# Cross-attention and mixture-of-experts layer: x^T by a second load and a block transpose on VectorE, layer norm 1 folded into the query weights and the exponential

## The chip, the cores and the metric

One core of a Trainium2 chip runs the kernel. The metric is the device time of one execution in microseconds (us); the profile is of one further execution. The engines are TensorE (PE, with its weight loads as PEld), VectorE (DVE), ScalarE (ACT), GpSimd (POOL) and SyncE (SP), which issues most DMAs. Each runs its own instructions in order and waits for the others by semaphores.

## The reference

There are 64 batches. A batch is x, 256 rows by 256 columns, and a context of 77 rows by 192. All is float32.

```python
def layernorm(x): return (x - mean(x)) / sqrt(var(x) + 1e-5)      # over the 256 columns

def cross_attention(x, context, Wq, Wk, Wv, Wo, bo):               # 8 heads of 64
    q, k, v = x @ Wq, context @ Wk, context @ Wv                   # split into heads
    attn = softmax((q @ k.T) * 64 ** -0.5)
    return (attn @ v) @ Wo + bo

def ffn(h, sim_matrix, gates, q_proj, k_proj, v_proj, o_proj):     # 16 experts of 64
    rw = gating(h, sim_matrix, gates)        # softmax over the experts that are on, at least the two best
    q, k, v = [sum_e rw[:, e] * (h @ proj[e]) for proj in (q_proj, k_proj, v_proj)]
    attn = softmax(causal(q @ k.T / 8)) @ v
    return sum_e (rw[:, e] * attn) @ o_proj[e]

x = x + cross_attention(layernorm(x), ctx, ...)
x = x + ffn(layernorm(x), ...)
```

## The kernel before

A product of two float32 matrices is made as three fast ones: each operand is split in a high half (rounded, written by ScalarE with a copy) and a low half (VectorE subtracts the high half from the source), and TensorE adds lo x hi, hi x lo and hi x hi (`product`, L577). Keys and values are folded into weights for three batches at a time: `gq` is the query weight times the keys of each head (jobs `g`, from `wq` and jobs `k`), `uo` the values times Wo (jobs `u`, from jobs `v`), so that the scores of a batch are xn @ gq and its cross-attention output is probs @ uo. These go through DRAM (`g_dram`, `u_dram`).

The main loop has steps i = 1 to 65. In step i the attention of batch i + 1 runs (scores S0 to S3, softmax, transposes PT0 to PT2 of the probabilities, output Y), the first half of the expert projections of batch i, the second half and the causal attention of batch i - 1, and the last product of batch i - 2. Each engine has its own list of this work, written by hand (`step` in each block), so the order on each queue is fixed.

Layer norm 1 of batch i + 2 (`nxt`) also runs in step i. VectorE takes mean and variance of the loaded tile `xt` (`ln1_a`), GpSimd raises the variance to the power -0.5 (`power`, L1822) and makes the shift, ScalarE writes the normalised rows `xn` (`ln1_b`, L1152, into the memory of `probs`; instructions L1149), TensorE transposes them in four pieces in slot XT (`a_xT`, L645; instructions L649) into PSUM, ScalarE copies the high half from there (L1021) and VectorE subtracts the low half (L1419). SP loads `xt` with one DMA (L412).

Slots of TensorE's work for attention and for the jobs share three PSUM banks in turn, in the order of `A_ORDER` (L42): E0, S0 to S3, E1, E2, PT0, PT1, PT2, E3, M1, XT, M2, M3, Y, L1, L2. A slot waits (`freed`, L588) until the slot three places back has been read out. So M2 gets the bank of E3, PT2 that of E2, and Y that of XT. Which job stands in a slot depends on i % 3 (`JOBS`, L44): E1 holds a `k` job for i % 3 == 2, which ScalarE reads out with four copies (L1036 to L1039) and VectorE with two subtractions (L1433), and a `g` or `u` job else, with one copy (L1082, L1105) and one subtraction (L1460, L1466). M3 holds a job (`ct`, the context's transpose) for i % 3 == 1 alone.

The expert projections are `b_qkv` j = 0 to 15; their blocks are accumulated by VectorE (L1541), or for the first two by ScalarE (L1142). The sum of attention and residual is VectorE's `a_y` (L1493). The causal attention's last product is `c_pv` on TensorE, into bank_c; it needs the low half of the transposed probabilities, VectorE's `c_pT` (L1547). The row maximum of the scores is taken by VectorE (`a_s`, L1471); ScalarE makes the 16 exponentials of a batch (`a_exp`, L1112), four a block, with the maximum as bias. `c_mix` (L1582) scales the attention output for all experts, and GpSimd subtracts its low half (L1915). GpSimd adds the bias `bo` to the rows of x (`a_xb`, L1842).

## Time and profile before

| | us |
|---|---|
| median of 3 runs | 2549.08 (2548.26 to 2549.45) |
| the profiled execution | 2547.88 |
| its span, first to last instruction | 2546.1 |

The span is followed in slices of 1/40. Each digit below is the busy share of a slice in tenths (9 is 90% or more); PEclk is the granted clock of TensorE in tenths of full speed; DMA is the mean busy share of the 16 DMA engines.

```profile
PE   5799999999999999999999999999999999999997
PEld 5799999999999999999999999999999999999997
DVE  6788888888888888888888888888888888888885
ACT  6666666666666666666666666666666666666642
POOL 2244444444444444444444444444444444444442
PEclk8899999999999999999999999999999999999998
DMA  6765556465565556466565556465565556465531
```

Times in the profile are us from the start of the span unless marked ns. In the rows "idle before" is how long the engine had stood, and the name behind the arrow is what ended that. The work is even from the third slice to the last but one. A share is a mean over stages with different limits.

### The profile page before, as it was taken

How to read it: one execution, taken by the hardware profiler on the slowest of the kernel's cores; microseconds unless marked ns; L12 is line 12 of the kernel's file. 1: busy time of each engine (PE TensorE's matmuls, PEld its weight loads, DVE VectorE, ACT ScalarE, POOL GpSimd, SP SyncE). 2: the span in 40 equal slices, each digit the busy share in tenths (PEclk: the TensorE clock that was granted, in tenths of full speed). 3: DMA queues.
4: the chain of work that ended last, by engine and by line, in shares of the span. 5: the costliest groups of instructions: out<-in, count | busy, mean ns of one | idle time of the engine just before them, and what ended most of it. 6: DMA issues, size and time to landing. Idle time of an engine off the chain costs nothing.

```text
span 2546.1 us, 54414 instructions
## 1 busy us (share of the span) xinstructions
PE 2477.4 (97%) x17308; PEld 2427.1 (95%) x17308; DVE 2124.1 (83%) x6126; ACT 1584.3 (62%) x5126; POOL 1104.3 (43%) x1741
## 2 busy tenths in 40 slices
PE   5799999999999999999999999999999999999997
PEld 5799999999999999999999999999999999999997
DVE  6788888888888888888888888888888888888885
ACT  6666666666666666666666666666666666666642
POOL 2244444444444444444444444444444444444442
PEclk8899999999999999999999999999999999999998
DMA  6765556465565556466565556465565556465531
GB/s 180 232 184 178 170 164 197 153 198 184 163 188 178 169 165 197 153 198 183 163 189 177 170 165 197 148 203 182 165 189 176 170 165 197 154 194 180 162 108 46
DMA packets 288070, 441.48 MB, mean 173 GB/s; under 512 B 20356, under 2 KB 199492, under 8 KB 279723
## 3 DMA queue, kind: packets, MB, share of 16 engines
q1 hardware_dynamic: 218155, 369.84, 44.6%
q10 hardware_dynamic: 69632, 68.17, 11.1%
q8 instruction: 140, 2.29, 0.4%
q14 instruction: 143, 1.17, 0.1%
HBM read 254.86 MB, written 181.83 MB: 172 GB/s over the span
## 4 chain that ended last, share of the span: by engine, by line
PE 81%; DVE 7%; POOL 5%; issue 3%; ACT 3%; DMA 0%; POOLq 0%; SPq 0%; DVEq 0%; ACTq 0%
PE bank_b L581 12%; PE bank_b L582 12%; PE bank_b L583 12%; PE bank_c L581 5%; PE bank_c L582 5%; PE bank_c L583 5%; PE bank_a L581 4%; PE bank_a L582 4%; PE bank_a L583 4%; PE bank_a L726 3%; PE bank_a L690 2%; PE bank_a L702 2%; DVE both L1433 2%; PE bank_a L691 1%; PE bank_a L665 1%
## 5 line engine op out<-in xcount | busy, mean ns | idle before, releaser
L1541 DVE SCALAR_TENSOR_TENSOR acc<-bank_b,rw,acc 128x192 f32<-128x192 f32 x1792 | 653.2, 408 | 108.9 <-PE bank_b L583 106.6
L581 PE MATMUL bank_b<-wqkv_hi,x2T_lo 128*128 128x384 f32 (+1 forms) x2048 | 721.3, 352 | 3.0 <-ACT acc L1142 1.6
L582 PE MATMUL bank_b<-wqkv_lo,x2T_hi 128*128 128x384 f32 (+1 forms) x2048 | 694.4, 339 | 0.0
L583 PE MATMUL bank_b<-wqkv_hi,x2T_hi 128*128 128x384 f32 (+1 forms) x2048 | 690.4, 337 | 0.0
L1915 POOL TENSOR_TENSOR mixs_lo<-mix,mixs_hi 128x512 fp32r<-128x512 f32 x254 | 378.2, 1520 | 164.5 <-ACT mixs_hi L1220 164.5
L1112 ACT ACTIVATE probs<-bank_a,s_max 128x77 f32<-128x77 f32 x1024 | 317.9, 331 | 202.3 <-DVE s_max L1471 202.3
L581 PEld LDWEIGHTS bank_b<-wqkv_hi,x2T_lo 128*128 128x128 f32 x2048 | 387.0, 189 | 5.4 <-ACT acc L1142 2.2
L582 PEld LDWEIGHTS bank_b<-wqkv_lo,x2T_hi 128*128 128x128 f32 x2048 | 387.5, 189 | 0.0
L583 PEld LDWEIGHTS bank_b<-wqkv_hi,x2T_hi 128*128 128x128 f32 x2048 | 385.5, 188 | 0.0
L1220 ACT ACTIVATE mixs_hi<-mix 128x512 fp32r<-128x512 f32 x256 | 159.8, 633 | 208.8 <-DVE mix L1582 208.8
L581 PE MATMUL bank_c<-wo_hi,mixs_lo 128*128 128x256 f32 x1000 | 281.2, 281 | 3.7 <-POOL mixs_lo L1915 3.7
L582 PE MATMUL bank_c<-wo_lo,mixs_hi 128*128 128x256 f32 x1000 | 280.5, 280 | 0.0
L583 PE MATMUL bank_c<-wo_hi,mixs_hi 128*128 128x256 f32 x1000 | 280.3, 280 | 0.0
L1908 POOL TENSOR_TENSOR probs<-probs,p_sum 128x616 f32<-128x616 f32 x128 | 156.1, 1220 | 249.7 <-DVE p_sum L1478 249.7
L1582 DVE TENSOR_TENSOR mix<-rw_all,late_tiles 128x512 f32<-128x512 f32 x256 | 245.9, 1000 | 20.3 <-ACT late_tiles L1214 20.3
L1889 POOL TENSOR_TENSOR mix<-acc 128x192 f32<-128x192 f32 x128 | 76.1, 595 | 377.9 <-DVE acc L1541 377.9
L1832 POOL TENSOR_TENSOR pow_out<-pow_in,expo 128x2 f32<-128x2 f32 (+1 forms) x128 | 111.3, 869 | 243.6 <-DVE pow_in L1391 227.2
L1112 ACT ACTIVATION_READ_ACCUMULATOR probs<-bank_a,s_max 128x1 f32 x1024 | 215.0, 210 | 0.0
L581 PEld LDWEIGHTS bank_c<-wo_hi,mixs_lo 128*128 128x128 f32 x1000 | 189.2, 189 | 3.8 <-issue 3.8
L582 PEld LDWEIGHTS bank_c<-wo_lo,mixs_hi 128*128 128x128 f32 x1000 | 189.2, 189 | 0.0
L583 PEld LDWEIGHTS bank_c<-wo_hi,mixs_hi 128*128 128x128 f32 x1000 | 189.1, 189 | 0.0
L581 PE MATMUL bank_a<-uo,pT_lo 128*128 128x256 f32 x630 | 177.3, 281 | 0.2 <-DVE xT_lo L1419 0.2
(262 smaller groups left out, 6389.7 us busy)
## 6 DMA issues: line engine op xcount, KB each, us to landing
gq<-g_dram SPq DMA_DIRECT2D x63, 1232.0 KB, 5.7
rw_all<-rw_dram ACTq DMA_DIRECT2D x128, 512.0 KB, 6.8
uo<-u_dram SPq DMA_DIRECT2D x63, 1024.0 KB
g_dram<-draft SPq DMA_DIRECT2D x103, 462.0 KB
u_dram<-draft SPq DMA_DIRECT2D x127, 308.0 KB
g_dram<-mixs_lo SPq DMA_DIRECT2D x63, 462.0 KB
xt<-in_x_dram SPq DMA_DIRECT2D x64, 256.0 KB, 4.7
out_dram<-mix SPq DMA_DIRECT2D x62, 256.0 KB, 4.0
```

Source lines behind the costliest of these rows:

```text
L581: nc.tensor.matmul(dst, lhs[1], rhs[0], start=start, stop=False)
L582: nc.tensor.matmul(dst, lhs[0], rhs[1], start=False, stop=False)
L583: return nc.tensor.matmul(dst, lhs[0], rhs[0], start=False, stop=stop)
L726: last = nc.tensor.transpose(bank_pt(n, k)[0:rows, col * P:(col + 1) * P], probs[:, t, chunk * P:chunk * P + rows], ident[:, :])
L1112: last = nc.scalar.activation(probs[:, t, h * NC:(h + 1) * NC], bank_s(n, j)[:, k * NC:(k + 1) * NC], ACT.Exp, bias=s_max[:, j, k:k + 1], ...
L1220: nc.scalar.activation(mixs[0][:, 2 * j:2 * j + 2, :], mix[:, 2 * j:2 * j + 2, :], copy).then_inc(mix_hi, 1)
L1541: V.scalar_tensor_tensor(acc[:, t, k, :], src, rw[:, t, e:e + 1], acc[:, t, k, :], ALU.mult, ALU.add).then_inc(b_evac, 1)
L1582: V.tensor_tensor(mix[:, 2 * j:2 * j + 2, :], rw_all[:, 2 * j:2 * j + 2, :], aT2[:, :].unsqueeze(1).to_broadcast([P, 2, T]), ALU.mult).the ...
L1832: G.tensor_tensor(dst, src, expo[:, 0:m], ALU.pow).then_inc(ln_pow[k], 1)
L1889: G.tensor_tensor(qkv[:, t, :], acc[:, t, 0, :], acc[:, t, 1, :], ALU.add).then_inc(qkv_ready, 1)
L1908: G.tensor_tensor(part, part, p_sum[:, half, 1, :, :].unsqueeze(3).to_broadcast([P, NT, HB, NC]), ALU.mult).then_inc(p_ready, 1)
L1915: G.tensor_tensor(mixs[1][:, 2 * j:2 * j + 2, :], mix[:, 2 * j:2 * j + 2, :], mixs[0].bitcast(F32)[:, 2 * j:2 * j + 2, :], ALU.subtract).t ...
```

## The change

x^T no longer comes from TensorE. SP loads x a second time with four DMAs of 64 KB (`load_blocks`), so that partitions 32k to 32k + 31 hold the rows s, s + 32, ... of the k-th quarter of the columns; the pieces are 64 columns (256 B) long. VectorE's transpose of 32 x 32 blocks (`a_blocks`) turns this tile into x^T in SBUF (`x_cols`), where even columns come first and odd ones second; Wq is loaded in the same order of rows. ScalarE's copy and VectorE's subtraction then read SBUF, not PSUM. Both stand later in the step: the block transpose behind `c_s`, the copy behind `b_exp`, the subtraction behind `a_y`. The loads stand between slots E2 and E3 on SP and wait for PT2's transposes, since they go into the memory of `probs`.

Layer norm 1 is no longer applied to x. Its mean goes into the query weights: each column of `wq` is centred, once at the start (four sums and four multiplies on VectorE, a bias in ScalarE's copies). Its deviation becomes a factor of the scores of a row: (var + eps) x 64 to the power -0.5 is the scale of the exponential, a column of SBUF, and one more multiply on VectorE scales each maximum. `ln1_b` and the shift on GpSimd are gone. Slot XT has no work and holds no bank; Y now waits for PT2's.

```diff
+        x_cols, x_later = [probs[:, :, :].rearrange("p t c -> p (t c)")[:, s * CC * T:(s + 1) * CC * T] for s in range(2)]
+        TB = T // 32
+        x_first = x2_first[:, :, :].rearrange("p t c -> p (t c)")
...
             def load_x(n):
                 if n:
                     sp.wait_ge(xb_ready, at(1, n - 1, 0))
-                    sp.wait_ge(ln_done[0], at(NT, n - 1, NT - 1))
+                    sp.wait_ge(ln_stats[0], at(2 * NT, n - 1, NT - 1))
...
+            def load_blocks(n):
+                if n > 1:
+                    sp.wait_ge(pt_fill, at(3, n - 1, 2))
+                for k in range(4):
+                    sp.dma_start(x_blocks(n)[k * 32:(k + 1) * 32, :].rearrange("p (k c) -> p k c", k=TB),
+                                 x[n, :, :].rearrange("(k s) c -> s k c", s=32)[:, :, k * C // 4:(k + 1) * C // 4]).then_inc(xt_in[n % 2], 16)
...
                 turn(i, "E2")
+                if on(i + 2):
+                    load_blocks(i + 2)
                 turn(i, "E3")
...
-            def a_xT(n):
-                pe.wait_ge(ln_done[0], at(NT, n, NT - 1))
-                for cc in range(CC):
-                    for t in range(NT):
-                        last = nc.tensor.transpose(bank_xt(n)[:, cc * T + t * P:cc * T + (t + 1) * P],
-                                                   xn[:, t, cc * P:(cc + 1) * P], ident[:, :])
-                last.then_inc(xt_fill, 1)
...
                 turn(i, "M1")
-                fill("XT", nxt, a_xT)
                 turn(i, "M2")
...
             def query_weights():
                 for k in range(HB):
                     act.wait_ge(wq_fill, k + 1)
-                    nc.scalar.activation(wq[:, 2 * k:2 * k + 2, :].rearrange("p a b -> p (a b)"), (banks_b[1:3] + banks_c)[k][:, :], copy,
-                                         scale=SCALE).then_inc(wq_hi, 1)
+                    act.wait_ge(wq_mean_ready, k + 1)
+                    for e in range(2):
+                        last = nc.scalar.activation(wq[:, 2 * k + e, :], (banks_b[1:3] + banks_c)[k][:, e * C:(e + 1) * C], ACT.Identity,
+                                                    bias=wq_mean[:, 2 * k + e:2 * k + e + 1])
+                    last.then_inc(wq_hi, 1)
 
             def a_xT(n):
                 act.wait_ge(xt_fill, at(1, n, 0))
-                nc.scalar.activation(xT[0][:, :, :].rearrange("p a b -> p (a b)"), bank_xt(n)[:, :], copy).then_inc(xt_hi, 1)
+                if n:
+                    act.wait_ge(s_fill, at(2 * NT, n - 1, 2 * NT - 1))
+                nc.scalar.activation(xT[0][:, :, :].rearrange("p a b -> p (a b)"), x_cols, copy).then_inc(xt_hi, 1)
...
-                                                bias=s_max[:, j, k:k + 1], accum_out=p_sum[:, half, 0, t, k:k + 1])
+                                                bias=s_max[:, j, k:k + 1], scale=pow_out[0][:, 0, t:t + 1], accum_out=p_sum[:, half, 0, t, k:k + 1])
...
                 do(ahead, a_pT, 2)
-                do(nxt, ln1_b)
                 turn(i, "E3")
                 do(now, b_xT, 0)
                 do(now, b_xT, 1)
                 turn(i, "M1")
-                do(nxt, a_xT)
                 do(before, c_qk)
                 turn(i, "M2")
                 do(before, c_exp)
                 do(now, b_exp)
+                do(nxt, a_xT)
                 turn(i, "M3")
...
             def query_weights():
                 for k in range(HB):
+                    dve.wait_ge(wq_fill, k + 1)
+                    mean = wq_mean[:, 2 * k:2 * k + 2]
+                    V.tensor_reduce(mean, (banks_b[1:3] + banks_c)[k][:, :].rearrange("p (e c) -> p e c", e=2), AX.X, ALU.add,
+                                    negate=True).then_inc(wq_sum, 1)
+                    dve.wait_ge(wq_sum, k + 1)
+                    V.tensor_scalar(mean, mean, 1.0 / C, None, ALU.mult).then_inc(wq_mean_ready, 1)
...
-                V.tensor_scalar(minus[k][:, :], mv[k][:, :, 0], -1.0, None, ALU.mult).then_inc(ln_var[k], 1)
                 if k == 0:
-                    V.tensor_scalar(pow_in[k][:, 0, :], mv[k][:, :, 1], EPS, None, ALU.add).then_inc(ln_var[k], 1)
+                    V.tensor_scalar(pow_in[k][:, 0, :], mv[k][:, :, 1], EPS, float(D), ALU.add, ALU.mult).then_inc(ln_var[k], 1)
...
+            def a_blocks(n):
+
+                dve.wait_ge(xt_in[n % 2], 64 * (n // 2 + 1))
+                if n:
+                    dve.wait_ge(pt_fill, at(3, n - 1, 2))
+                V.transpose(x_cols.rearrange("p (a k s) -> p a k s", a=CC, k=TB),
+                            x_blocks(n).rearrange("p (k r a) -> p a k r", k=TB, a=CC)).then_inc(xt_fill, 1)
+
             def a_xT(n):
                 hi, lo = flat(xT, slice(None), slice(None), slice(None))
                 dve.wait_ge(xt_hi, at(1, n, 0))
-                V.tensor_tensor(lo, bank_xt(n)[:, :], hi.bitcast(F32), ALU.subtract).then_inc(xt_evac, 1)
+                V.tensor_tensor(lo, x_cols, hi.bitcast(F32), ALU.subtract).then_inc(xt_evac, 1)
...
-                                negate=True).then_inc(s_max_ready, 1)
+                                negate=True).then_inc(s_top, 1)
+                dve.wait_ge(ln_pow[0], at(1, n, 0))
+                dve.wait_ge(s_top, at(2 * NT, n, j))
+                V.tensor_scalar(s_max[:, j, :], s_max[:, j, :], pow_out[0][:, 0, j % 2:j % 2 + 1], None, ALU.mult).then_inc(s_max_ready, 1)
...
                 turn(i, "M1")
-                do(nxt, a_xT)
                 do(now, b_z, 0)
...
                 do(before, c_s)
+                do(nxt, a_blocks)
                 do(before, c_p)
...
                 do(now, b_wsum)
                 turn(i, "M2")
                 do(ahead, a_y)
+                do(nxt, a_xT)
                 turn(i, "M3")
                 do(before, c_pT)
```

## Rows read from the trace of the kernel before

**Rows 1.** The page: busy us of each engine (share of the span), instructions.

```profile
PE 2477.4 (97%) x17308; PEld 2427.1 (95%) x17308; DVE 2124.1 (83%) x6126; ACT 1584.3 (62%) x5126; POOL 1104.3 (43%) x1741
```

**Rows 2.** Three steps: us, busy of PE, PEld, DVE, ACT, POOL, clock, DMA, GB/s.

```profile
974.00:1088.59 114.59, 114.15 (x809) 112.18 (x808) 97.60 (x285) 72.89 (x238) 51.48 (x81) 1.00 0.57 177
```

**Rows 3.** Timeline of PE around slot XT: start, us, line, out<-in.

```profile
1050.19 0.60 PE L649 MATMUL bank_a<-ident,probs 128*128 128x128 f32 x4
1050.84 0.37 PE L665 MATMUL bank_a<-cT_hi,wv_lo 128*128 128x232 f32 x1
```

**Rows 4.** Timeline of DVE in the same stretch; idle before in brackets.

```profile
1049.45 0.74 DVE L1541 SCALAR_TENSOR_TENSOR acc<-bank_b,rw,acc 128x192 f32<-128x192 f32 x2 [0.55 <-PE bank_b L583]
...
1050.11 0.68 DVE L1466 TENSOR_TENSOR mixs_lo<-bank_a,mixs_lo 116x512 fp32r<-116x512 f32 x1
```

**Rows 5.** Waits of PE's weight loads, 400 to 2400: total us, times, longest.

```profile
PEld bank_a L665 <- DVE mixs_lo L1460: 9.5, 36, 0.3
...
PEld bank_a L665 <- DVE mixs_lo L1466: 5.0, 17, 0.3
PEld bank_c L581 <- DVE mixs_lo L1547: 4.9, 17, 0.3
```

**Rows 6.** Timeline of DVE, second half of the step i % 3 == 0.

```profile
1019.02 0.17 DVE L1571 RECIPROCAL p_sum<-p_sum 128x2 f32<-128x2 f32 x1 [0.71 <-ACT mix L1185]
1019.22 0.60 DVE L1575 TENSOR_SCALAR mix<-mix,p_sum 128x128 f32<-128x128 f32 x2
1020.38 0.19 DVE L1527 TENSOR_REDUCE w_sum<-w 128x2 f32<-128x32 f32 x1 [0.55 <-POOL w L1874]
...
1021.50 0.69 DVE L1493 TENSOR_TENSOR late_tiles<-bank_a,xb 128x512 f32<-128x512 f32 x1
1022.27 0.56 DVE L1547 TENSOR_TENSOR mixs_lo<-bank_c,mixs_lo 128x384 fp32r<-128x384 f32 x1
```

**Rows 7.** One line's instructions: duration ns min/median/max.

```profile
L1582 DVE TENSOR_TENSOR mix<-rw_all,late_tiles x256: 682/693/1782, 145.8 to 2535.1; 128x512 f32<-128x512 f32 x128
```

**Rows 8.** Timeline of PE: the first product of c_pv in that step.

```profile
1023.13 0.28 PE L581 MATMUL bank_c<-mixs_lo,mixs_hi 128*128 128x256 f32 x1
```

**Rows 9.** ACT's groups by form: busy us, mean ns of one | idle before.

```profile
L1142 ACT ACTIVATE acc<-bank_b,rw 128x192 f32<-128x192 f32 x256 | 94.2, 425 | 99.4 <-POOL rw L1880 99.4
...
L1127 ACT ACTIVATE x2T_hi<-bank_b 128x256 fp32r<-128x256 f32 x128 | 42.3, 382 | 53.1 <-PE bank_b L763 53.1
L1021 ACT ACTIVATE xT_hi<-bank_a 128x512 fp32r<-128x512 f32 x64 | 38.0, 593 | 0.2 <-PE bank_a L649 0.2
```

**Rows 10.** Timeline of ACT, exponentials and E1, step i % 3 == 2.

```profile
1074.73 0.33 ACT L1112 ACTIVATE probs<-bank_a,s_max 128x77 f32<-128x77 f32 x1 [1.02 <-DVE s_max L1471]
...
1077.81 0.33 ACT L1112 ACTIVATE probs<-bank_a,s_max 128x77 f32<-128x77 f32 x1 [0.51 <-DVE s_max L1471]
...
1079.03 1.09 ACT L1149 ACTIVATE mix<-late_tiles,shift,pow_out 128x256 f32<-128x256 f32 x2
1080.29 0.36 ACT L1036 ACTIVATE only<-bank_a 64x231 fp32r<-64x231 f32 x1 [0.17 <-PE bank_a L669]
```

**Rows 11.** Timeline of DVE: E2's subtraction in the same step.

```profile
1083.89 0.63 DVE L1460 TENSOR_TENSOR mixs_lo<-bank_a,mixs_lo 128x462 fp32r<-128x462 f32 x1
```

**Rows 12.** Timeline of PE: transposes of slot PT2 in the same step.

```profile
1084.71 0.60 PE L726 MATMUL bank_a<-ident,probs 128*128 128x128 f32 x4
```

**Rows 13.** Timeline of DVE behind slot E1, step i % 3 == 1.

```profile
1044.73 0.74 DVE L1541 SCALAR_TENSOR_TENSOR acc<-bank_b,rw,acc 128x192 f32<-128x192 f32 x2 [0.81 <-PE bank_b L583]
```

**Rows 14.** The page's DMA queues: packets, MB, share of 16 engines.

```profile
q1 hardware_dynamic: 218155, 369.84, 44.6%
```

**Rows 15.** Timeline of SP's queue: issue of one load.

```profile
1061.76 0.40 SPq L412 DMA_DIRECT2D xt<-in_x_dram  x1
```

**Rows 16.** Timeline of PE in the opening: first use of the query weights.

```profile
21.61 0.35 PE L690 MATMUL bank_a<-both,wq 128*128 128x232 f32 x1 [2.90 <-issue]
```

**Rows 17.** Timeline of POOL behind the residual sum.

```profile
1060.44 1.30 POOL L1842 TENSOR_TENSOR xb<-xt,bo_all 128x512 f32<-128x512 f32 x1 [1.25 <-DVE late_tiles L1493]
```

81 lines of the change are left out of this document (37 added, 44 removed).

## The prediction

> **What bounds the kernel now.** I read the page's busy shares first: TensorE is busy for 97% of the span and VectorE for 83% [rows 1]. Then a window over three steps of the steady loop, since the work repeats with a period of three: 114.59 us, 38.20 a step, TensorE busy 114.15 of it at the full clock [rows 2]. So TensorE sets the end, and the change takes work from it. What it can give back must be read on TensorE's own timeline, at the place where the work goes, because a queue in order gives nothing back if its next instruction waits for something that is no earlier.
>
> **The four transposes, removed in 61 steady steps.** In the step shown they start at 1050.19 and the next product (L665, slot M2) starts at 1050.84 [rows 3], so the slot is worth 0.65 us, or 61 x 0.65 = 39.7 us at most. But the slots share three PSUM banks in turn: M2 gets the bank of E3 and waits until VectorE has subtracted that. That subtraction (L1466) starts at 1050.11 and lasts 0.68, so it ends at 1050.79 [rows 4], 0.05 before L665 starts. It follows the two accumulations of block 15, which themselves had waited 0.55 for TensorE [rows 4], so it is tied to a product ahead of the removed slot. The waits agree: within 2000 us the weight load of L665 waited for this subtraction 36 + 17 = 53 times, up to 0.3 us each [rows 5], which is every one of some 52 steps. The transposes stand in a hole that stays when they go. I credit 0.06 us a step (the longer start after a transpose), 61 x 0.06 = 3.7 us; bounds 0 and 39.7.
>
> **VectorE's subtraction that makes the low half, moved.** Before, it ran ahead of the router's maxima, where VectorE waits for TensorE. Now it stands right behind the residual sum (L1493) and ahead of the subtraction L1547, on which TensorE's product with V waits. In a step without context work L1493 starts at 1021.50 and L1547 at 1022.27, lasting 0.56 [rows 6]. The new one has two SBUF sources of 512 columns like L1582, whose shortest is 0.682 and median 0.693 [rows 7]; with the usual overlap of 0.08 it holds the engine for 0.61. L1547 then starts at 1021.50 + 0.61 + 0.61 = 1022.72 and ends at 1023.28, and the product, which started at 1023.13 [rows 8], starts near 1023.34 with a slower second one behind: +0.28 us. In the third of the steps that has context work in slot M3, L1547 is already the last to arrive (17 waits of up to 0.3 [rows 5]); so the whole 0.60 is added. Sum: 40 x 0.28 + 21 x 0.60 = 23.8 us. Lower bound 0, if something else on VectorE goes earlier; upper bound from the longest L1582, 1.782: 1.1 more in each of 61 steps, 67 us.
>
> **The exponential's scale.** Each of the 16 exponentials of a batch takes its scale from a column of SBUF instead of a constant. No row has this form. Nearest: L1142, 192 columns with such a scale, takes 425 ns, while L1127, 256 columns without, takes 382 [rows 9]; with L1021, 512 columns in 593 [rows 9], a column is 0.82 ns, 192 plain ones 329, and a scale column costs about 0.09 us (bounds 0 and 0.10). The maximum gets a multiply behind it that waits for it: L1571 to L1575, such a pair, are 0.20 us apart [rows 6], so each maximum reaches ScalarE 0.21 us later, and the fourfold adds 0.8 us a step to VectorE. In the step shown the second block of exponentials starts at 1074.73, the last at 1077.81 after an idle 0.51, and the layer norm behind them at 1079.03 [rows 10]. Now: second block at 1074.73 + 0.42 = 1075.15, then 12 exponentials by 0.39 in a row, 1079.86, so 0.83 later. Slot E1's copies started at 1080.29 after 0.17 of waiting for TensorE [rows 10], so they start 0.66 later. In steps of type i % 3 == 2 four copies stand there, VectorE waits for them and then has no gap until E2's subtraction, L1460 at 1083.89 for 0.63, end 1084.52 [rows 11]. TensorE's transposes PT2 need that bank and start at 1084.71 [rows 12]. With 0.07 from the end of a subtraction to its release the rest, 0.59 us, is a new wait: 20 x 0.59 = 11.8 us. In the other two types E1 has one copy, and behind it VectorE waits 0.81 for TensorE [rows 13], so nothing. Bounds 0 (no cost of the scale column) and 61 x 0.66 = 40 us.
>
> **VectorE's block transpose.** No row shows one. From below, one pass over 512 columns, the 0.68 of L1582; from above two passes, 1.35. I take 0.68, as its neighbours with 512 columns all take one pass. It stands behind c_s, where VectorE idles 0.71 before L1571 [rows 6]: nothing at 0.68, and up to 1.2 is covered in two of three types by its next wait, 0.55 for GpSimd (L1527) [rows 6]. ScalarE's copy to the high half moves behind b_exp, where that engine waits for GpSimd's weights: free. The normalising pair on ScalarE (L1149 on probs) goes, 1.08 us a step, from a place where the engine then waits for TensorE: no gain.
>
> **The second load.** 4 DMAs of 64 KB, 1024 pieces of 256 B a batch. Queue 1 spent 44.6% of 16 x 2546 us on 218155 packets [rows 14], 83 ns each at 1.7 KB, so at most 1024 x 83 / 16 = 5.3 us, and half of that if a packet's time goes down with its size. On SP the wait for PT2 holds back slot E3's store and what follows; an issue is 0.40 [rows 15], 1.6 for four, and E3's store is due only 4 us later. From PT2 (1085) to the block transpose one step on (1056.8 + 38.2 = 1095) are 10 us; issue, transfer and landing need 5 to 8. Free, with 2 us to spare. The Trainium skill (DMA: Bandwidth & Descriptors, Specifications) wants at least 512 B a transfer for line rate, with a read-modify-write below that; no row here shows such a load. By the rows it adds nothing to the sum, by that rule it comes nearer to its deadline, and past it the late-load rival below holds.
>
> **The opening.** Before the first use of the query weights (L690 at 21.61 [rows 16]) VectorE now makes four sums over 512 columns. At L1582's 0.69 [rows 7] and with the dependent multiply this is 0.81 a head pair, 3.3 us, with ScalarE's two copies in place of one hidden behind. The block transposes ahead of the copies of batches 0 and 1 add 0.5, their 32 longer exponentials (0.09 each) 2.7, and the missing normalisation gives back 1.0: +5.5 us (bounds 2 and 9).
>
> **The sum** against the profiled execution, 2547.88 us (span 2546.1 and 1.8 around it): -3.7 + 23.8 + 11.8 + 5.5 = +37.4, so 2585.3. The median of the runs is 1.2 above the profiled execution: **2586 us**, 1.4% slower.
>
> **The rivals.**
> Faster (0.13): the hole ahead of M2 closes, because E3's subtraction gets earlier by the 0.65. For it speaks that ScalarE loses 1.08 us just before E3's copy; against it that VectorE's accumulations ahead of it waited for TensorE. It decides at an end of L1466 by 1050.2 in the frame shown. With the new waits hidden too, 2549.1 - 39.7 + 5.5 = 2515 us (0.10); if they stay, 2515 + 23.8 + 11.8 = 2550 (0.03).
> Waits hidden, nothing gained (0.13): the subtraction's place and the scale column cost nothing on TensorE, only the opening counts: 2549.1 + 5.5 - 3.7 = 2551, or up to 2556 with a remnant. For it: the slack is misread by no more than 0.3 us a step.
> Port collision (0.10): the moved subtraction reads two SBUF tensors while GpSimd adds the bias to x (L1842, 1.30 us from 1060.44 [rows 17]), started by the same residual sum. L1582 shows the effect: 0.68 alone, 1.782 at worst beside GpSimd [rows 7]. In my sum VectorE is first, since its instruction follows without a gap. If GpSimd is first, up to 61 x 1.1 = 67 us more: 2653; with half of them 2620. The Trainium skill (SBUF — State Buffer, Who interferes with whom) calls the shared port pair an exclusive lock, taken by whoever starts first; by it, too, the order decides.
> Late load (0.06): the pieces land after the block transpose's turn, and VectorE stands, with the softmax's normalisation and the router's sum queued behind. 1 us a step would be 61 us, 2647.
> The forecast (0.58), with its own range of 2566 to 2606.
>
> **How the numbers follow.** The range must leave out no more than 2 in 10: it starts at 2549, above the faster rival (0.10) and an edge of the mixed form (0.02), and ends at 2615, leaving out half of the two last rivals (0.08). Faster by over 0.2% (about what a measurement of this kernel can tell from no change) comes from the first rival less its mixed form: 0.10. Within 0.2% (2544 to 2554): that mixed form and most of the hidden case, 0.13. Slower: 0.77.
>
> **What would show it.** The weight load of M2's product waits for E3's subtraction for some 0.7 us instead of 0.3. The product with V (bank_c) waits for L1547's successor in all steps, 0.3 to 0.9. In every third step PT2's transposes wait 0.6 for E2's subtraction. The exponentials stand 0.39 apart instead of 0.30. The block transpose takes 0.68 and VectorE never waits for the load. The first product with query weights starts near 25. I am wrong if M2 starts 0.6 earlier behind M1, if the product with V starts without a wait, or if VectorE or the load shows waits that I have not named.

## The result and the profile after

| | median of 4 runs, us | range |
|---|---|---|
| before | 2548.67 | 2546.77 to 2549.45 |
| after | 2634.56 | 2631.22 to 2636.62 |

The ratio is 1.034, with a 95% interval from 1.032 to 1.035: 86 us slower. The prediction was 2586 us, slower by 37, with 2615 as the upper end. The side was right, the size was not.

The page of the kernel after: busy us of each engine (share of the span), and its DMA queue 1.

```profile
PE 2489.9 (95%) x17052; PEld 2407.0 (92%) x17052; DVE 2183.6 (83%) x6390; ACT 1617.4 (62%) x5002; POOL 1109.4 (42%) x1677
...
q1 hardware_dynamic: 287659, 386.64, 47.5%
```

TensorE has 256 instructions fewer than in [rows 1] and yet falls from 97% to 95% of a longer span: it waits more. The page also follows the chain of work that ended last, from each instruction back to what released it. First the kernel before, then the kernel after, shares of the span:

```profile
PE 81%; DVE 7%; POOL 5%; issue 3%; ACT 3%; DMA 0%; POOLq 0%; SPq 0%; DVEq 0%; ACTq 0%
```

```profile
PE 35%; DVE 30%; issue 10%; ACT 9%; DMA 7%; POOL 5%; SPq 3%; DVEq 0%; ACTq 0%; POOLq 0%
```

Before, TensorE alone carried the chain; now VectorE carries nearly as much of it, and the loads 7%. The line numbers have moved: the product is now L598 to L600 (L581 to L583 before), E1's and E2's subtractions L1467, L1473 and L1440 (L1460, L1466, L1433), the one for the product with V L1557 (L1547), the transposes PT L732 (L726), the first products of M2 L671 (L665), the exponentials L1118 (L1112). New are the block load L423, the block transpose L1420, the moved subtraction L1426 and the multiply on the maxima L1482.

To find where the time went I laid a mark in every step, VectorE's residual sum (L1503, L1493 before), and read the stretches between two marks, windows of both kernels: us, busy of PE, PEld, DVE, ACT, POOL, clock, DMA, GB/s. First the kernel before. The stretches end in steps with i % 3 = 2, 0 and 1.

```profile
945.03:983.38 38.35, 38.18 (x271) 37.25 (x269) 32.81 (x97) 24.29 (x81) 17.14 (x27) 1.00 0.58 179
983.38:1021.50 38.12, 37.92 (x268) 37.25 (x268) 32.42 (x95) 24.13 (x81) 17.17 (x27) 1.00 0.56 171
1021.50:1059.60 38.10, 38.03 (x271) 37.65 (x271) 32.37 (x93) 24.46 (x81) 17.15 (x27) 1.00 0.58 182
```

And the same three of the kernel after.

```profile
981.53:1021.70 40.17, 38.44 (x264) 36.94 (x264) 33.91 (x100) 25.25 (x80) 17.21 (x26) 1.00 0.60 178
1021.70:1060.18 38.48, 37.81 (x264) 36.88 (x264) 33.23 (x98) 24.56 (x79) 17.26 (x26) 1.00 0.62 177
1060.18:1099.55 39.37, 38.45 (x267) 37.33 (x267) 33.12 (x98) 24.70 (x77) 17.25 (x26) 1.00 0.62 181
```

The first kind of stretch grows by 1.8 us, the second by 0.4, the third by 1.3. The clock is full in all of them. Over the run the mark of batch 3 comes at 196.38 instead of 180.84 (+15.5), from there to batch 60 there are 2243.11 instead of 2177.84 (+65.3), and from batch 60 to the last 115.27 instead of 111.49 (+3.8). Who makes TensorE wait in the steady part is seen in the waits of its weight loads, 400 to 2400: total us, times, longest.

```profile
PEld bank_a L671 <- DVE mixs_lo L1467: 22.3, 34, 0.7
PEld bank_c L598 <- DVE mixs_lo L1557: 21.4, 49, 0.6
PEld bank_a L708 <- DVE both L1440: 19.5, 34, 0.8
PEld bank_a L732 <- DVE mixs_lo L1467: 12.9, 17, 0.8
PEld bank_a L671 <- DVE mixs_lo L1473: 10.2, 17, 0.7
PEld bank_a L732 <- DVE both L1440: 8.4, 33, 0.7
```

Not all of this is new. Of the same list in the kernel before, one more row is needed beside [rows 5], the u jobs' (L702 there):

```profile
PEld bank_a L702 <- DVE both L1433: 7.7, 19, 0.6
```

L671 (slot M2) waits up to 0.7 instead of 0.3, which is the removed slot's time turned into waiting; the product with V (L598, bank_c) waits in nearly every step, not in every third; L732 (PT1 and PT2) waits for E1's and E2's subtractions, which it did not before; and L708 (the u jobs) waits 19.5 instead of 7.7, where the new part is slot L1's wait for M2's subtraction. M2's, PT2's and the product with V's were forecast, those of PT1 and L1 were not.

A new wait on VectorE tells why slot L1 is late. First SP's queue in the step whose block transpose is shown behind it, with i % 3 = 1, then VectorE, then TensorE at slot L1.

```profile
1047.59 1.88 SPq L423 DMA_DIRECT2D probs<-in_x_dram  x4
...
1085.21 0.80 SPq L451 DMA_DIRECT2D u_dram<-mixs_lo  x2
1086.06 4.99 SPq L423 DMA_DIRECT2D probs<-in_x_dram  x4
...
1097.18 0.71 DVE L1420 STREAM_TRANSPOSE probs<-probs 128x512 f32<-128x512 f32 x1 [1.23 <-DMA probs<-in_x_dram]
...
1098.73 0.78 DVE L1440 TENSOR_TENSOR both<-bank_a,only 64x231 fp32r<-64x231 f32 x2
...
1099.66 0.34 PE L708 MATMUL bank_a<-wo,both 128*116 128x256 f32 x1 [0.48 <-DVE both L1440]
```

The first row is the same load one step earlier, where no such stores stand ahead: 1.88 us for the four issues. Here they stand behind two stores of `u_dram` and take 4.99, where I had counted 1.6, and VectorE stands for 1.23 us until they have landed. In 17 such steps the four issues take 3.4 to 5.7 us, 4.5 in the middle; in the steps with i % 3 = 0 it is 1.8. Everything behind is late with it, down to the subtraction L1440 for which slot L1 waits.

### The profile page after: what moved, and what is told of

Read it like the earlier page. It is cut to its first block, busy times and chain, and to the rows that moved or that the text cites. A ratio compares the mean times of both kernels' runs of the same rounds, so it can differ in the third digit from the quotient of the medians.

```text
span 2629.4 us, 54494 instructions
## 1 busy us (share of the span) xinstructions
PE 2489.9 (95%) x17052; PEld 2407.0 (92%) x17052; DVE 2183.6 (83%) x6390; ACT 1617.4 (62%) x5002; POOL 1109.4 (42%) x1677
## 3 DMA queue, kind: packets, MB, share of 16 engines
q1 hardware_dynamic: 287659, 386.64, 47.5%
## 4 chain that ended last, share of the span: by engine, by line
PE 35%; DVE 30%; issue 10%; ACT 9%; DMA 7%; POOL 5%; SPq 3%; DVEq 0%; ACTq 0%; POOLq 0%
DVE acc L1551 8%; DMA probs<-in_x_dram 7%; PE bank_b L598 5%; PE bank_b L600 5%; PE bank_b L599 5%; DVE mix L1592 3%; DVE both L1440 3%; PE bank_c L598 3%; ACT probs L1118 3%; SPq L423 3%; PE bank_c L600 2%; PE bank_c L599 2%; DVE s_max L1478 2%; DVE s_max L1482 2%; ACT mix L1161 2%
## 5 line engine op out<-in xcount | busy, mean ns | idle before, releaser
L598 PE MATMUL bank_b<-wqkv_hi,x2T_lo 128*128 128x384 f32 (+1 forms) x2048 | 721.9, 353 | 3.2 <-ACT acc L1148 1.7
L600 PE MATMUL bank_b<-wqkv_hi,x2T_hi 128*128 128x384 f32 (+1 forms) x2048 | 693.3, 339 | 0.0
L1118 ACT ACTIVATE probs<-bank_a,s_max,pow_out 128x77 f32<-128x77 f32 x1024 | 410.3, 416 | 203.1 <-DVE s_max L1482 201.0
L598 PEld LDWEIGHTS bank_b<-wqkv_hi,x2T_lo 128*128 128x128 f32 x2048 | 387.8, 189 | 10.1 <-ACT acc L1148 6.7
L600 PEld LDWEIGHTS bank_b<-wqkv_hi,x2T_hi 128*128 128x128 f32 x2048 | 385.7, 188 | 0.0
L598 PE MATMUL bank_c<-wo_hi,mixs_lo 128*128 128x256 f32 x1000 | 282.3, 282 | 3.7 <-POOL mixs_lo L1930 3.7
L600 PE MATMUL bank_c<-wo_hi,mixs_hi 128*128 128x256 f32 x1000 | 283.9, 284 | 0.0
L1118 ACT ACTIVATION_READ_ACCUMULATOR probs<-bank_a,s_max,pow_out 128x1 f32 x1024 | 208.7, 204 | 0.0
L598 PEld LDWEIGHTS bank_c<-wo_hi,mixs_lo 128*128 128x128 f32 x1000 | 189.7, 190 | 3.9 <-issue 3.8
L600 PEld LDWEIGHTS bank_c<-wo_hi,mixs_hi 128*128 128x128 f32 x1000 | 188.5, 188 | 0.0
L1440 DVE TENSOR_TENSOR both<-bank_a,only 64x231 fp32r<-64x231 f32 x352 | 137.9, 392 | 47.6 <-ACT both L1045 43.7
```

Source lines behind the costliest of these rows:

```text
L598: nc.tensor.matmul(dst, lhs[1], rhs[0], start=start, stop=False)
L600: return nc.tensor.matmul(dst, lhs[0], rhs[0], start=False, stop=stop)
L1118: last = nc.scalar.activation(probs[:, t, h * NC:(h + 1) * NC], bank_s(n, j)[:, k * NC:(k + 1) * NC], ACT.Exp, bias=s_max[:, j, k:k + 1], ...
L1440: last = V.tensor_tensor(both[rows, k, e, cols], src[rows, cols], only.bitcast(F32)[rows, k, e, cols], ALU.subtract)
```

## The experiments

Each kernel was timed beside the kernel before, on the same chip. A gain is first that of the medians against 2634.56, which was measured apart from them. The profiled execution of the kernel after was 3.3 us below its median, so between profiled spans (after: 2629.4) most gains are some 3 us smaller. Neither column is surer than a few us: the four executions of the kernel after lie 5.4 us apart.

| kernel | median, us | against after | span, us | against after |
|---|---|---|---|---|
| early_load | 2611.8 | -22.8 | 2610.0 | -19.4 |
| early_mid | 2596.1 | -38.4 | 2594.2 | -35.2 |
| late_sub | 2668.2 | +33.6 | 2666.8 | +37.4 |
| plain_exp | 2594.9 | -39.6 | 2594.7 | -34.7 |
| mult_only | 2611.1 | -23.4 | 2612.3 | -17.1 |
| psum_late | 2618.2 | -16.4 | 2616.5 | -12.9 |
| no_centre | 2626.7 | -7.9 | 2626.2 | -3.2 |
| stripped | 2558.4 | -76.2 | 2556.5 | -72.9 |

### One transpose of four in slot XT, in the kernel before

```diff
                     for t in range(NT):
+                        if n > 2 and (cc, t) != (0, 0):
+                            continue
                         last = nc.tensor.transpose(bank_xt(n)[...], xn[...], ident[:, :])
```

> The kernel before, from batch 3 on with one of slot XT's four transposes instead of four; ScalarE and VectorE read the bank as it is, so three quarters of x^T are not made. Theory 1, a hole (slot M2 must wait for VectorE's subtraction of E3, wherever TensorE stands): nearly nothing comes back, 0 to -4 us, 2545 to 2549. Theory 2, the slot is worth its length: three transposes are 0.45 to 0.5 us, 61 times, -27 to -30 us, 2519 to 2522.

2548.0 us, ratio 1.000 (0.999 to 1.001). Theory 1. The waits of TensorE's weight loads in that kernel, 400 to 2400 (the product at M2 is L667 here):

```profile
PEld bank_a L667 <- DVE mixs_lo L1462: 20.5, 36, 0.6
PEld bank_a L667 <- DVE mixs_lo L1468: 10.6, 17, 0.6
```

In [rows 5] the same two were 9.5 and 5.0 with 0.3 as the longest. 16.6 us of waiting have come where three transposes were, and the end does not move. In the step of [rows 3] the product of M2 starts 0.66 us behind the start of slot XT with one transpose (1051.06 to 1051.72), and 0.65 with four.

### The block loads ahead of E2's stores

```diff
-                turn(i, "E2")
                 if on(i + 2):
                     load_blocks(i + 2)
+                turn(i, "E2")
```

> The kernel after, with the four block loads issued ahead of slot E2's stores instead of behind them. Theory 1 (they land late because they queue behind the u stores, and VectorE's wait of about 1 us in steps with i % 3 = 1 makes slot L1 wait 0.63 for M2's subtraction): the wait for the load goes, -13 us, 2621. Theory 2 (slot L1 waits because the block transpose itself stands ahead of M2's subtraction): no change, 2632 to 2636. Theory 3 (the stores behind the loads are now late in turn, and a draft's release holds back ScalarE): slower.

2611.8 us, 22.8 less. Theory 1, and more than it had said. VectorE's waits for the load between 400 and 2400, total us, times, longest, in the kernel after and then in this one:

```profile
DVE probs L1420 <- DMA probs<-in_x_dram: 23.6, 23, 2.4
```

```profile
DVE probs L1420 <- DMA probs<-in_x_dram: 2.6, 5, 0.9
```

SP's queue in a step with i % 3 = 1 of this kernel:

```profile
1080.39 2.63 SPq L423 DMA_DIRECT2D probs<-in_x_dram  x4
```

The stores of `u_dram` from E2 follow at 1083.07. The four issues take 2.1 to 3.0 us in such steps, instead of 3.4 to 5.7, and they no longer stand behind those stores' own issues. From the first issue to the last landing it is 9.9 us in the middle, instead of 10.8. The stretches that end in steps with i % 3 = 1 shrink from 39.4 to 38.7 us on average, the two other kinds change by less than 0.1. So this cost lies in the order of SP's queue, not in the bytes: all the loads are still there.

### VectorE's subtraction one place later

```diff
                 do(ahead, a_y)
-                do(nxt, a_xT)
                 turn(i, "M3")
                 do(before, c_pT)
+                do(nxt, a_xT)
```

> The kernel after, with VectorE's subtraction for the low half of x^T one place later, behind the subtraction that the product with V waits for. Theory 1 (it stands in that product's way, 0.33, 0.23 and 0.35 us in three steps looked at): -0.3 us in each of 61 steps, -18 us, 2616, and the product starts without a new wait. Theory 2 (the product is late because the whole of VectorE's list is, by the block transpose and the multiplies): less than 5 us, 2630 or above.

2668.2 us: slower by another 33.6, which neither theory had. The wait of the product with V for L1557 is gone from the list, as theory 1 said. The timeline of VectorE and GpSimd around the moved subtraction, in this kernel:

```profile
1038.87 0.56 DVE L1557 TENSOR_TENSOR mixs_lo<-bank_c,mixs_lo 128x384 fp32r<-128x384 f32 x1
...
1038.94 1.29 POOL L1857 TENSOR_TENSOR xb<-xt,bo_all 128x512 f32<-128x512 f32 x1 [1.25 <-DVE x_first L1503]
...
1039.35 1.43 DVE L1426 TENSOR_TENSOR xT_lo<-probs,xT_hi 128x512 fp32r<-128x512 f32 x1
```

And in the kernel after:

```profile
1022.31 0.68 DVE L1426 TENSOR_TENSOR xT_lo<-probs,xT_hi 128x512 fp32r<-128x512 f32 x1
...
1022.54 1.60 POOL L1857 TENSOR_TENSOR xb<-xt,bo_all 128x512 f32<-128x512 f32 x1 [1.25 <-DVE x_first L1503]
...
1022.91 0.55 DVE L1557 TENSOR_TENSOR mixs_lo<-bank_c,mixs_lo 128x384 fp32r<-128x384 f32 x1
...
1023.53 0.19 PEld L598 LDWEIGHTS bank_c<-mixs_lo,mixs_hi 128*128 128x128 f32 x1 [0.36 <-DVE mixs_lo L1557]
```

The moved subtraction (L1426) has two inputs in SBUF, and so has GpSimd's addition (L1857). Whoever starts first runs at its own pace: VectorE 0.68 and GpSimd 1.60 in the kernel after, GpSimd 1.29 and VectorE 1.43 here. That is the port collision of my rivals, met by an edit that had another purpose. In the kernel after VectorE never pays for it (all 64 subtractions take 0.68 to 0.69). Here every one of the steady part is longer, 1.29 on average, so 0.61 x 61 = 37 us more on VectorE, and 33.6 by the medians, 37.4 by the spans, reach the end. The match of the sums doesn't show that VectorE's time counts one to one: by kind of stretch (ending in i % 3 = 0, 1 and 2) it is 0.5, 1.3 and 0.1 us. The Trainium skill (SBUF — State Buffer, Who interferes with whom) says that the shared port pair goes to whoever issues first, and that VectorE with two inputs in SBUF contends with GpSimd's reads; the trace agrees.

### The same subtraction behind the accumulations 2 and 3

This stands on top of early_load's edit.

```diff
                 do(ahead, a_y)
-                do(nxt, a_xT)
                 turn(i, "M3")
                 do(before, c_pT)
                 do(now, b_qkv, 2)
                 do(now, b_qkv, 3)
+                do(nxt, a_xT)
```

> The kernel after with the block loads ahead of slot E2's stores (which gave 2611.8) and with VectorE's subtraction for the low half of x^T two places later still than in the run before, behind the accumulations of expert projections 2 and 3, where GpSimd's addition of the bias has ended (1.3 us from 1038.94; the subtraction one place later fell beside it and took 1.43 instead of 0.68). Theory 1 (in late_sub it was this collision alone that cost time): the subtraction takes 0.68, the product with V no longer waits, -0.3 in each of 61 steps, 2593. Theory 2 (VectorE's and ScalarE's own chain from the residual sum to the exponentials sets slots E1 to PT2, and TensorE only moves its wait there): 2605 to 2612.

2596.1 us, 15.7 less than early_load alone and 38.4 less than after. Theory 1, 3 us short of its 2593. The subtraction takes 0.68 again, and of the 21.4 us of waiting of the product with V (26.2 in early_load) this row of the kernel's waits is left, about that of [rows 5]:

```profile
PEld bank_c L598 <- DVE mixs_lo L1557: 4.7, 15, 0.4
```

Part of the wait has moved, as theory 2 had it: L732's (PT1 and PT2) for L1440 grows from 8.4 us in early_load to 14.7, and for L1473 from 1.1 to 4.3.

### A constant scale and no multiply on the maxima

```diff
-   bias=s_max[:, j, k:k + 1], scale=pow_out[0][:, 0, t:t + 1], accum_out=...
+   bias=s_max[:, j, k:k + 1], scale=1.0, accum_out=...
...
-   V.tensor_scalar(s_max[:, j, :], s_max[:, j, :], pow_out[0][:, 0, j % 2:j % 2 + 1], None, ALU.mult)
```

> The kernel after, with a constant 1.0 as the exponential's scale and no multiply on the maxima; layer norm's deviation and the factor 1/8 are left out of the scores. Theory 1 (the longer exponentials and the later maxima push slot E1's four copies, and TensorE waits twice in steps with i % 3 = 2, for E1's subtraction 0.58 and for E2's 0.66): -1.24 us in 20 steps and some 3 us in the opening, -28 us, 2607. Theory 2 (E1 is late by what stands behind it on VectorE, not by ScalarE): under 10 us, 2625 or above.

2594.9 us, 39.6 less: theory 1, again with a larger size. PT2's wait for E2's subtraction (12.9 us) is gone, and PT's for E1's is down from 8.4 to 2.8. The exponentials, this kernel's and then those of the kernel after: busy us, mean ns of one | idle before.

```profile
L1118 ACT ACTIVATE probs<-bank_a,s_max 128x77 f32<-128x77 f32 x1024 | 317.9, 330 | 204.9 <-DVE s_max L1478 204.9
```

```profile
L1118 ACT ACTIVATE probs<-bank_a,s_max,pow_out 128x77 f32<-128x77 f32 x1024 | 410.3, 416 | 203.1 <-DVE s_max L1482 201.0
```

The column costs 0.086 us each, the 0.09 of the prediction. The gain is not the scale's alone: in the steps with i % 3 = 1 the loads land 0.5 us earlier behind the step's mark, and VectorE's wait for them falls from 23.6 to 13.1 us between 400 and 2400.

### The multiply kept, the column away

```diff
-   scale=pow_out[0][:, 0, t:t + 1]
+   scale=1.0
...
-   V.tensor_scalar(s_max[:, j, :], s_max[:, j, :], ...)
+   V.tensor_scalar(s_spare[:, j, :], s_max[:, j, :], ...)
```

> The kernel after with a constant 1.0 as the exponential's scale, but with the multiply still behind each maximum: its result goes to memory that nothing reads, the exponentials wait for it as before. Layer norm's deviation and the factor 1/8 are left out of the scores. plain_exp, without both, gave 2594.9. Theory 1 (the scale column costs most: 16 times 0.085 us on ScalarE a batch): 2598 to 2607. Theory 2 (the multiply costs most: 0.23 us and a wait behind each maximum, and up to 0.87 where GpSimd is in the way): 2618 to 2630.

2611.1 us, between the two theories. The column is worth 17 us by the spans and 23 by the medians, the multiply 2611.1 - 2594.9 = 16.2 (17.6 by the spans). These shares hang on the order in which the two are taken away: with the column gone, ScalarE stands 0.74 ahead of the last block of exponentials, waiting for its maximum, where it stands 0.16 in the kernel after. I looked at each multiply. In the kernel after, VectorE's last one of a batch and GpSimd beside it, and further down the slots that follow in this step with i % 3 = 2:

```profile
997.87 0.23 DVE L1482 TENSOR_SCALAR s_max<-s_max,pow_out 128x4 f32<-128x4 f32 x1
...
1000.29 1.22 POOL L1923 TENSOR_TENSOR probs<-probs,p_sum 128x616 f32<-128x616 f32 x1 [2.22 <-DVE p_sum L1488]
...
1000.67 0.87 DVE L1482 TENSOR_SCALAR s_max<-s_max,pow_out 128x4 f32<-128x4 f32 x1
...
1005.63 0.81 DVE L1440 TENSOR_TENSOR both<-bank_a,only 64x231 fp32r<-64x231 f32 x2 [1.46 <-ACT both L1045]
...
1006.49 0.43 PE L732 MATMUL bank_a<-ident,probs 128*104 128x128 f32 x2 [0.26 <-DVE both L1440]
1008.41 0.66 PE L732 MATMUL bank_a<-ident,probs 128*128 128x128 f32 x4 [0.45 <-DVE mixs_lo L1467]
```

The fourth multiply, of four elements a partition, takes 0.87 and ends at 1001.54, with GpSimd's instruction at 1001.51. It is longer than 0.3 in 63 of 64 batches, and 0.8 or more in 60. GpSimd's normalising is started by VectorE's reciprocal two instructions earlier, so they always meet.

### The reciprocal behind the fourth maximum

```diff
-                do(ahead, a_psum, 0)
                 do(ahead, a_s, 3)
+                do(ahead, a_psum, 0)
```

> The kernel after, with VectorE's reciprocal of the first two blocks' sums (which starts GpSimd's normalising of the probabilities, 1.22 us) behind the fourth maximum and its multiply instead of ahead of them. In the kernel after the fourth multiply takes 0.87 instead of 0.23 and ends with GpSimd's instruction (1039.99 + 0.86 = 1040.85, 1039.61 + 1.22 = 1040.83). Theory 1 (they collide, and the last block of exponentials and slot E1's copies are late by it): all multiplies take 0.23, and in the steps with i % 3 = 2 some 0.6 goes from E1's and PT2's waits, 20 x 0.64 = 13 us, 2621; Theory 2 (the multiply is slow for a reason of its own, or the exponentials are late anyway): 2630 to 2636. Theory 3 (the normalised probabilities are now late for PT0): slower than 2638.

2618.2 us, 16.4 less, ratio to before 1.027 (1.025 to 1.028). Theory 1 in the collision and in the size: 255 of 256 multiplies take 0.23 now, and the gain, 12.9 to 16.4, is most of what the multiply cost. In its place theory 1 is right only in part. PT2's wait for E2's subtraction stays (12.7 us after 12.9); what shrinks is PT1's for E1's (8.4 to 3.6) and the u jobs' (19.5 to 15.5). The stretches that end in steps with i % 3 = 2 lose 0.26 us, which is near the 0.28 by which the last block of exponentials follows the third sooner, and those of i % 3 = 1 lose 0.42, which theory 1 did not have. There VectorE's wait for the load is a little shorter too (20.3 us in all, after 23.6); what the rest is was not tried. Nothing is left out here, only two entries of VectorE's list have changed places. By the Trainium skill (SBUF — State Buffer, Who interferes with whom) a `tensor_scalar` can use both ports of VectorE, and then whichever of the two engines issues first keeps the shared pair for its whole instruction; the trace agrees, for a multiply of 128 x 4.

### The query weights not centred

```diff
-   act.wait_ge(wq_mean_ready, k + 1)
-   for e in range(2): ... ACT.Identity, bias=wq_mean[...]
+   nc.scalar.activation(wq[:, 2 * k:2 * k + 2, :]..., copy, scale=1.0)
...
-   V.tensor_reduce(mean, ...); V.tensor_scalar(mean, mean, 1.0 / C, ...)
```

> The kernel after without the centring of the query weights (no sums and multiplies on VectorE, ScalarE's four copies as in the kernel before but with scale 1.0); the mean of layer norm 1 is left out. Theory 1 (the 3.2 us by which the first product with the query weights starts later are passed on, and TensorE's lower granted clock in 20 to 40 us, 0.54 against 0.83, is a result of the longer pause): 6 to 9 us less, 2626 to 2629. Theory 2 (only the pause itself): 3 us less, 2631.5. Theory 3 (the opening is late by the exponentials and the loads, not here): no change.

2626.7 us, 7.9 less by the medians, which would be theory 1; but the intervals of the two ratios touch (1.029 to 1.033 here, 1.032 to 1.035 after), and by the spans it is 3.2, theory 2. The trace speaks for theory 2: the mark of batch 3 comes 2.95 us earlier (193.43), and behind it the two kernels run alike. TensorE's first product with the query weights in the kernel after, then in this one:

```profile
24.77 0.53 PE L696 MATMUL bank_a<-both,wq 128*128 128x232 f32 x1 [6.76 <-issue]
```

```profile
21.38 0.35 PE L696 MATMUL bank_a<-both,wq 128*128 128x232 f32 x1 [2.83 <-issue]
```

The delay is 3.4 us. The granted clock of 20 to 40 us is 0.55 here and 0.54 in the kernel after (0.83 before), so the longer pause is not what lowers it, against theory 1. What does was not found; stripped, below, shows 0.50 there and before_one 0.83, so it comes with something that stripped still has and the kernel before has not.

### All new waits stripped

The edits of early_mid, plain_exp and no_centre together.

> The kernel after with all four edits at once: loads ahead of E2's stores, the subtraction behind the accumulations 2 and 3, constant scale and no multiply, no centring (the whole of layer norm 1 is left out). What is left of the change is that TensorE's transposes are gone and that the block load and VectorE's block transpose are there. Theory 1 (M2's wait for E3's subtraction eats the slot, as before_one showed on the kernel before): 2545 to 2556. Theory 2 (with the new waits gone the 0.65 us a step come back): 2508 to 2520. Theory 3 (the block transpose and the load have a price of their own): above 2560.

2558.4 us, ratio 1.004 (1.0025 to 1.0054). Theory 2 is out: with 76 us of new cost gone the kernel is still not faster than the kernel before. The waits of M2's weight loads, 400 to 2400:

```profile
PEld bank_a L671 <- DVE mixs_lo L1457: 23.7, 36, 0.7
PEld bank_a L671 <- DVE mixs_lo L1463: 12.0, 17, 0.7
```

It is 2 us above theory 1's range and 2 below theory 3's: some 3 us of the rest lie ahead of batch 3, 6 between batches 3 and 60 (0.1 a step). VectorE no longer waits for the load between 400 and 2400, but what of the rest belongs to the load and what to the block transpose was not tried apart. By the spans the single gains add up: 19.4 (load) + 15.8 (subtraction) + 34.7 (exponentials) + 3.2 (centring) = 73.1, against 72.9 together, and the rest is 2556.5 - 2546.1 = 10.4. That they add up doesn't make them independent: plain_exp alone already takes 10 us of VectorE's wait for the load. By the medians (22.8 + 15.7 + 39.6 + 7.9) they are 86.0 against 76.2; three of the four carry the 3.3 between the median and the profiled execution of the kernel after, the two together only once.

### Can the hole be closed?

TensorE's product E3 is subtracted by VectorE behind the accumulations of block 15, which wait for TensorE. Four kernels exchange the two:

```diff
-                do(before, b_qkv, 15)
                 turn(i, "E3")
+                do(before, b_qkv, 15)
                 do(now, b_xT, 0)
```

> The whole kernel before with that same exchange on VectorE alone. Theory 1 (M2 waits for E3's subtraction only as long as TensorE is busy with slot XT anyway): no change, 2545 to 2550. Theory 2 (the later accumulation of block 15 delays TensorE's next use of its bank or x2T): slower, above 2555.

> As before_one (the kernel before, one transpose of four in slot XT from batch 3 on, three quarters of x^T not made; 2548.0), and VectorE subtracts E3's product ahead of the accumulations of block 15 instead of behind them: ScalarE's copy that it needs ends at 1049.00 in the step shown, the subtraction would end near 1049.8 instead of 1050.79. Theory 1 (the hole ahead of M2 is this subtraction and nothing else): the three transposes now count, 61 x 0.45 = 27 us less, 2520 to 2525. Theory 2 (another release stands close behind, such as VectorE's later accumulation or ScalarE's copies): 2535 to 2549.

> early_mid (the kernel after with the loads ahead of E2's stores and the subtraction of x^T behind the accumulations 2 and 3; 2596.1) with the same exchange. Theory 1 (the 0.65 us a step of the removed transposes stand in the hole at M2): 61 x 0.5 to 0.65 = 30 to 40 us less, 2557 to 2566. Theory 2 (ScalarE's and VectorE's chain through the exponentials is the bound by now, and TensorE waits in E1 and PT2 for what it no longer waits for in M2): 2580 to 2596.

> stripped (2558.4: all of layer norm 1's new work left out, loads and subtraction in better places) with the same exchange. Theory 1 (the hole is E3's subtraction): 61 x 0.5 to 0.65 less, 2518 to 2528. Theory 2 (something else of the 0.65 is lost): above 2540.

| kernel | without the exchange | with it | ratio to before, with it |
|---|---|---|---|
| before | 2547.65 | 2532.15 | 0.993 (0.992 to 0.995) |
| before, one transpose | 2548.0 | 2532.14 | 0.994 (0.992 to 0.995) |
| early_mid | 2596.1 | 2583.1 | 1.014 (1.012 to 1.015) |
| stripped | 2558.4 | 2538.7 | 0.996 (0.995 to 0.998) |

None of the four came out by its theory 1. That of before_swap was wrong to the kernel's advantage: the kernel before, whole, is 15.5 us faster than it was, and faster than every form of the change. Its M2 had waited in [rows 5], 0.3 at a time, and that is what comes back (0.2 a step). In one_swap, on top of the exchange, three missing transposes give nothing again; it lies between its theories, nearer to the second, whose other release close behind is in the trace. early_mid_swap is in the range of its theory 2, and stripped_swap, 11 us above its theory 1, just misses its theory 2. TensorE and GpSimd around M2 in one_swap:

```profile
1048.71 0.27 PE L651 MATMUL bank_a<-ident,probs 128*128 128x128 f32 x1
1048.74 0.35 PE L667 MATMUL bank_a<-cT_hi,wv_lo 128*128 128x232 f32 x1
...
1048.16 0.73 DVE L1543 SCALAR_TENSOR_TENSOR acc<-bank_b,rw,acc 128x192 f32<-128x192 f32 x2
...
1048.97 0.60 POOL L1891 TENSOR_TENSOR mix<-acc 128x192 f32<-128x192 f32 x1 [0.87 <-DVE acc L1543]
...
1049.71 0.41 PE L791 MATMUL bank_c<-ident,mix 128*128 128x128 f32 x2 [0.17 <-POOL mix L1891]
```

The hole ahead of M2 is closed: L667 follows the transpose by 0.03. It opens five products later, at `c_qk` (L791), which waits for GpSimd's sum, and that for VectorE's accumulation of block 15. In one_swap the weight loads of L791 wait 53 times, 17.4 us in all, in before_swap (L789) twice. In early_mid_swap and stripped_swap the same place (L795) waits 52 and 53 times, 23.8 and 22.3 us. The last kernel has all four moves and leaves nothing out:

> The kernel after with all four moves that keep the result: loads ahead of E2's stores, subtraction of x^T behind the accumulations 2 and 3, E3's subtraction ahead of block 15 (these three gave 2583.1), and the reciprocal behind the fourth maximum. Theory 1 (the collision's 0.64 us in 20 steps come back here too): 2570. Theory 2: 2580 to 2584.

2574.3 us, ratio 1.010 (1.008 to 1.011): 60 us better than the change as made, still 1% behind the kernel before. It is 8.8 less than early_mid_swap, so between the two theories.

## Why the prediction was right or wrong

**The bound, and the transposes removed (forecast -3.7, found 0).** Right. before_one and stripped show that the slot is a hole: the work goes and a wait of the same length takes its place. The faster rival with the new waits hidden was 2515; stripped, which has these waits taken out, ended at 2558, close to the 2551 to 2556 that I had for hidden waits and nothing gained. That the hole would open again at the next place once it was closed I had not seen.

**The subtraction moved (forecast +23.8, found 15.8).** The mechanism was right, the product with V waits in nearly all steps, 0.3 to 0.6. The size was too large by 8: in every third step I added the whole 0.60 to a wait that was there, and it grew from 0.29 to 0.58 on average. The order of the collision rival fell on the cheap side, as I had argued, and late_sub shows the price of the other one, 33.6 us where I had written up to 67.

**The exponential's scale (forecast +11.8 and 2.7 of the opening, found 34.7 to 39.6). This is the first step that failed.** By the spans 6.6 of the 34.7 lie ahead of batch 3's mark, so 28.1 stand against the 11.8. The column's 0.09 was right (its own rows give 0.096, it measured 0.086), and PT2 does wait in every third step (17 times, 0.76 on average). I had 0.59 there; from the end of L1460 at 1084.52, the release of 0.07 and the start at 1084.71 it should have been 0.54. That wait is 12.9 us of 2000 and so about the size of my term; the rest of the cost is outside it. What failed is first the multiply: I priced it at 0.20 from a pair of small instructions and did not ask what runs on GpSimd at its place. The fourth one meets the normalising and takes 0.87, just where the last block of exponentials waits for it. psum_late gives 13 to 16 us back by taking that collision away. I had looked for this collision for the large subtraction alone. Second is the cover, where I had put every other step at nothing: E1's own subtraction, later too, holds PT1's last transposes in the same steps. The column alone, at 17 us by the spans (14 of them between batches 3 and 60, 3 ahead of them), was already worth more than my whole term, since it acts in the stretches of the third kind too (39.4 to 38.9 us on average without it), where I had found cover. A part of it goes by way of the loads: without the column VectorE waits 15.7 us for them instead of 23.6.

**The block transpose (forecast 0, and 0.68 long).** Its length was right: 0.70 to 0.715. Its place was right in two of three kinds of step; where the load is late it hands that on.

**The second load (forecast 0, found 19.4 to 22.8). The second step that failed.** My 10 us from PT2 to the block transpose were about right, and issue to landing was 7.0 us in the median of single DMAs. From the first issue to the last landing it was 10.8 in the steps with i % 3 = 1, where I had 5 to 8. The failing figure in it is 1.6 us for four issues. It came from one row, a load with pieces of 1 KB [rows 15]. Behind the stores of the u jobs the four took 3.4 to 5.7. I had asked what queues behind the loads, not what they queue behind. As a rival it had 0.06 and 1 us a step; it came in every third step and a few more, 23 times in 2000 us, at 1.0 us on average and 2.4 at most. The rule of the Trainium skill on transfers under 512 B (DMA: Bandwidth & Descriptors, Specifications) was not what decided, though by rate the trace doesn't speak against it: queue 1 spent 47.5% of 16 x 2629.4 us, some 1810 us more than in [rows 14], on 69504 more packets, 26 ns each. That is a third of the mean packet's 83 ns, but for 0.24 KB against 1.7, so about twice the time a byte. It makes 1.8 us a batch on each of 16 engines (an estimate), and early_load, with the same transfers, has nearly no wait.

**The opening (forecast +5.5, found 15.5).** The first product came at 24.77, as forecast (near 25). Of the 15.5 us by the mark of batch 3 plain_exp gives back 6.6 (189.75) and no_centre 3.0; in stripped 3.0 are left. Of the 6.6 the column has 2.8 (193.61 in mult_only), and I had 2.7 for it; the multiplies have the other 3.9, and I had not counted them. The lower clock between 20 and 40 us is left unexplained.

**The sum.** By the spans 0 + 15.8 + 34.7 + 19.4 + 3.2 = 73.1 are accounted for by single edits, of 83.3 (2629.4 - 2546.1), with the overlap of exponentials and load said above. The remaining 10 are in stripped, not further divided. The scale term lies inside the bounds that I had given it, 0 to 40; the load had no bounds in the sum, only its rival. Each of the two missed by about 20 us, so the upper end of my range, 2615, had room for one of them and not for both. The multiply and the load failed in one way: a price was taken from a quiet row, and its neighbours on the port or the queue were not read. The column's price was right, and its cover was misread.

## What to carry to other kernels

Removing work from the busiest engine gives nothing where its next instruction waits for something tied to another chain; read what releases the instruction behind the gap, and the one behind that, before crediting any of it. A small instruction added to a chain must be priced with what the engine that shares its port is doing at that moment, and a transfer with what stands ahead of it in its queue. And when a trace shows a wait of 0.3 us in every step at the bound, look for a neighbour to exchange: exchanging two lines in VectorE's list brought 15.5 us, where taking three transposes from TensorE brought nothing.

## What the runs showed of the hardware

A `tensor_scalar` of 4 elements a partition on VectorE that fell beside GpSimd's normalising ended with it (0.87 instead of 0.23), and a subtraction of 512 columns with two inputs in SBUF took 1.43 instead of 0.68 behind the start of GpSimd's addition. A scale from an SBUF column makes an exponential of 77 columns 0.086 us longer (416 against 330 ns). A block transpose of 128 x 512 float32 takes 0.71 us, little more than the 0.68 of a subtraction over 512 columns. Four DMA issues of 64 KB in pieces of 256 B take SP 1.8 us with no store just ahead and 3.4 to 5.7 behind the stores of `u_dram`.
